# Attention pooling on one core: TensorE's loop from chunk 4 to the last, own places for two high halves of the odd chunks, and one softmax for the last two chunks

## The reference

```python
h = relu(einsum('bse,eh->bsh', behavior_emb, W_b) + (candidate_emb @ W_c)[:, None, :] + fc1_b)
scores = einsum('bsh,h->bs', h, fc2_w[:, 0]) + fc2_b[0]
attn = softmax(scores, axis=-1)
user_interest = einsum('bse,bs->be', behavior_emb, attn)
x = concatenate([user_interest, candidate_emb], axis=1)
logit = (relu(x @ mlp1_w + mlp1_b) @ mlp2_w + mlp2_b)[:, 0]
```

## Time and profile before

| | us |
|---|---|
| median of 3 runs | 272.15 (271.59 to 272.36) |
| the profiled execution | 271.89 |
| its span | 270.1 |
| TensorE busy in it | 255.4 (95%) |
| VectorE, ScalarE, GpSimd busy | 208.7, 198.1, 28.9 |

### The profile page before, as it was taken

How to read it: one execution, slowest core, us unless ns; L and a number is a source line. 1 busy time by engine, 2 the same in 40 slices (tenths; PEclk the granted TensorE clock), 3 DMA queues, 4 the chain that set the end, 5 groups by cost and what they waited for, 6 DMA issues and landing times.

```text
span 270.1 us, 10363 instructions
## 1 busy us (share of the span) xinstructions
PE 255.4 (95%) x3942; PEld 213.1 (79%) x3942; DVE 208.7 (77%) x321; ACT 198.1 (73%) x481; POOL 28.9 (11%) x38
## 2 busy tenths in 40 slices
PE   8979798979989999999999999999999999979995
PEld 7547677868778888888888988888888888868864
DVE  1448977958779797979899797979798897966441
ACT  2657975948859696978969696978879696966311
POOL 2000202011020110202020110202020101102100
PEclk9999999999999999999999999999999999999999
DMA  7999999999999999999999999999999999999200
GB/s 246 434 428 425 426 423 421 425 423 427 423 425 428 425 427 427 425 425 427 425 428 427 425 430 425 427 428 430 425 428 425 425 427 427 420 429 408 110 0 3
DMA packets 10688, 105.87 MB, mean 392 GB/s; under 512 B 1200, under 2 KB 1712, under 8 KB 2864
## 3 DMA queue, kind: packets, MB, share of 16 engines
q1 hardware_dynamic: 10384, 105.44, 92.8%
q10 hardware_dynamic: 288, 0.20, 0.2%
HBM read 105.63 MB, written 0.00 MB: 391 GB/s over the span
## 4 chain that ended last, share of the span: by engine, by line
PE 87%; DMA 4%; issue 3%; DVE 2%; SPq 1%; ACT 1%; DVEq 0%; ACTq 0%
PE z_ps L670 18%; PE s_ps L687 17%; PE z_ps L674 16%; PE z_ps L671 16%; PE u_ps L699 16%; DMA xt<-in_behavior_t 4%; PE z_ps L699 1%; PE z_ps L741 1%; PE z_ps L784 1%; SPq L260 1%; PE z_ps L778 1%; ACT hidden_rest L408 1%; DVE xl L498 1%; SPq L264 0%; PE z_ps L765 0%
## 5 line engine op out<-in xcount | busy, mean ns | idle before, releaser
L498 DVE TENSOR_TENSOR xl<-xt,xh 128x800 fp32r<-128x800 f32 x120 | 115.8, 996 | 6.1 <-ACT xh L364 3.3
L364 ACT CAST xh<-xt 128x800 fp32r<-128x800 f32 x120 | 102.3, 917 | 13.7 <-PE z_ps L674 10.8
L670 PE MATMUL z_ps<-xh,w_hi 128*128 128x512 f32 x240 | 86.0, 358 | 3.7 <-ACT hidden_rest L408 1.8
L671 PE MATMUL z_ps<-xh,w_lo 128*128 128x512 f32 x240 | 79.4, 345 | 0.0
L408 ACT ACTIVATE hidden_rest<-z_ps,bias 128x200 f32<-128x200 f32 x192 | 67.5, 454 | 7.6 <-PE z_ps L674 5.8
L674 PE MATMUL z_ps<-xl,w_hi 128*128 128x512 f32 x240 | 63.4, 345 | 0.5 <-DVE xl L498 0.5
L670 PEld LDWEIGHTS z_ps<-xh,w_hi 128*128 128x128 f32 x240 | 45.1, 188 | 21.2 <-issue 10.0
L508 DVE TENSOR_TENSOR hidden_rest<-z_ps,neg_bias 128x800 f32<-128x800 f32 x48 | 47.4, 987 | 9.7 <-PE z_ps L674 7.2
L335 POOL TENSOR_TENSOR weights_by_row<-weights,masks_sb 128x400 f32<-128x400 f32 x31 | 27.1, 873 | 224.1 <-DVE xl L498 194.4
L699 PE MATMUL u_ps<-x,weights_by_row 128*32 128x128 f32 (+1 forms) x1680 | 45.3, 262 | 6.0 <-issue 6.0
L671 PEld LDWEIGHTS z_ps<-xh,w_lo 128*128 128x128 f32 x240 | 45.1, 188 | 5.5
(11 more groups left out here) (70 smaller groups left out, 93.7 us busy)
## 6 DMA issues: line engine op xcount, KB each, us to landing
x<-in_behavior SPq DMA_DIRECT2D x31, 1600.0 KB, 18.5
xt<-in_behavior_t SPq DMA_DIRECT2D x30, 1600.0 KB, 16.8
xt<-in_behavior_t SPq DMA_DIRECT2D x4, 400.0 KB, 4.9
xt<-in_behavior_t SPq DMA_DIRECT2D x2, 800.0 KB, 7.6
x<-in_behavior SPq DMA_DIRECT2D x1, 832.0 KB, 8.3
x<-in_behavior SPq DMA_DIRECT2D x1, 768.0 KB, 9.7
later_sb<-in_later SPq DMA_DIRECT2D x1, 258.5 KB, 19.6
first_sb<-in_cand_rest SPq DMA_DIRECT2D x1, 192.0 KB, 5.7
```

What stands on the lines that cost most here:

```text
L364: nc.scalar.copy(xh[g][:, :], xt[q][:, g, :]).then_inc(xh_made, 1)
L498: nc.vector.tensor_tensor(xl[g][:, :], xt[q][:, g, :], xh[g][:, :].bitcast(F32), ALU.subtract).then_inc(xl_made, 1)
L670: nc.tensor.matmul(z[:, a:b], w_hi[:, :], xh[g][:, a:b], start=True, stop=False)
L671: nc.tensor.matmul(z[:, a:b], w_lo[:, :], xh[g][:, a:b], start=False, stop=False)
```

## The change

- `FIRST` is 4 instead of 6, so the loop's body starts at chunk 4. `periods` takes the number of turns: seven on TensorE (chunks 4 to 31, nothing is left behind it), six on ScalarE and VectorE (4 to 27; 28 to 31 are written out).
- TensorE has no `LAST` phase any more. Behind the loop it does the row sums, a transposition, the scores of 30 and 31 together, the weighted sums of 28 and 29, and then the end. The softmax of 30 and 31 is one of seven steps.
- Period 4 now has a transposition too, of a `pooled4` that GpSimd clears at the start; `pooled_t` has two pairs of columns more, and the counts of semaphores move by two.
- `xh` has two tiles more: the third and fourth high halves of odd chunks go there, and ScalarE casts all four of an odd chunk in one run, ahead of the exponentials.
- At the end the transposition of the pair 28, 29 is between the two sets of candidates, and on VectorE the last mask comes ahead of `normalise(0)`.
- Three tiles of the end (`inv_sel`, `pooled_n`, `z_all`) lie in buffers of `xt` that are free by then.

```diff
-        xh = [sb(f"xh{i}", [P, WIDTH], F32R) for i in range(GROUPS)]
+        xh = [sb(f"xh{i}", [P, WIDTH], F32R) for i in range(GROUPS + 2)]
...
-        FIRST = 6
+        FIRST = 4
...
-        def periods(body):
+        def periods(body, turns):
             def run(eng):
                 for c in range(FIRST):
                     body(c, c % X_BUFS, c)
-                with eng.Fori(0, (CHUNKS - FIRST - 2) // X_BUFS) as turn:
+                with eng.Fori(0, turns) as turn:
                     for j in range(FIRST, FIRST + X_BUFS):
                         body(turn * X_BUFS + j, j % X_BUFS, FIRST)
-                body(LAST - 1, (LAST - 1) % X_BUFS, FIRST)
-                body(LAST, LAST % X_BUFS, LAST)
+                for c in range(FIRST + turns * X_BUFS, CHUNKS):
+                    body(c, c % X_BUFS, LAST if c == LAST else FIRST)
...
+        def xh_of(q, g):
+            return xh[g if g < 2 or q % 2 == 0 else g + 2]
...
+            nc.gpsimd.memset(pooled4[:, :], 0.0).then_inc(pooled4_copied, 2)
...
-                    act.wait_ge(z_done, c * GROUPS + (g + 1 - GROUPS))
+                    act.wait_ge(z_done, c * GROUPS + (g + 1 - (GROUPS if g < 2 else 2 * GROUPS)))
...
-                if phase > 1:
-                    high_half(c, q, 3, None, phase == WHOLE)
                 if q % 2 == 1:
                     next_half(0)
                     biased_relu(c, q, 1, phase)
...
+                high_half(c, q, 3, None, phase == WHOLE)
                 biased_relu(c, q, 1, phase)
-                next_half(0)
-                next_half(1)
+                for g in range(GROUPS):
+                    next_half(g)
                 for n in range(2):
                     exponents(c - 2 + n, n, pair_steps(c - 2) + 2 * (PAIR_STEPS - 1 + n), phase == 2)
                 if phase > 2:
                     copy_pooled4(c - X_BUFS + 1, u_ps)
-                next_half(2)
                 biased_relu(c, q, 3, phase)
-            periods(period)(act)
+            periods(period, (CHUNKS - FIRST) // X_BUFS - 1)(act)
+            copy_pooled_t(LAST - 4, u_ps[:, P:P + 2 * ROWS])
+            for n in range(2):
+                exponents(LAST - 1 + n, n, pair_steps(LAST - 1) + 2 * (PAIR_STEPS - 1 + n), False)
             copy_pooled4(LAST - 2, u_ps)
             copy_pooled_t(LAST - 2, u_ps[:, P:P + 2 * ROWS])
-            exponents(LAST, LAST % 2, IN_PAIRS + 4 * ALONE_STEPS, False)
...
-            for n in range(ALONE_STEPS):
-                softmax(LAST, 1, n, IN_PAIRS + 2 * ALONE_STEPS, False)
+            for n in range(PAIR_STEPS):
+                softmax(LAST - 1, n, False)
+            mask_last()
             normalise(0)
-            mask_last()
...
-                    if phase == LAST:
-                        transpose_sums(LAST - X_BUFS, beside_z(q, g))
-                        score(LAST - 1, (q - 1) % X_BUFS, pair_steps(LAST - 3) + 2)
-                        weighted_sum(LAST - 3, (q - 3) % X_BUFS, False)
...
-            periods(period)(pe)
+            periods(period, (CHUNKS - FIRST) // X_BUFS)(pe)
             pe.wait_ge(later_loaded, 16)
             row_sums(0)
-            weighted_sum(LAST - 2, (LAST - 2) % X_BUFS, False)
-            score(LAST, LAST % X_BUFS, IN_PAIRS + 2)
-            transpose_sums(LAST - 2, u_ps[:, P:P + 2 * ROWS])
-            spread_inverses(0)
-            for part in range(2):
-                for m in range(2):
-                    mlp_candidates(part, m)
+            transpose_sums(LAST - 4, u_ps[:, P:P + 2 * ROWS])
+            score(LAST - 1, (LAST - 1) % X_BUFS, pair_steps(LAST - 3) + 2)
+            score(LAST, LAST % X_BUFS, None)
+            pe.wait_ge(pooled_t_copied, LAST - 1)
+            weighted_sum(LAST - 3, (LAST - 3) % X_BUFS)
+            weighted_sum(LAST - 2, (LAST - 2) % X_BUFS)
+            spread_inverses(0)
+            for m in range(2):
+                mlp_candidates(0, m)
+            transpose_sums(LAST - 2, u_ps[:, P:P + 2 * ROWS])
+            for m in range(2):
+                mlp_candidates(1, m)
             row_sums(1)
             weighted_sum_alone(LAST - 1)
```

More of the change, by code:

```diff
@@ L360, in high_half @@
                 if not early:
-                    act.wait_ge(z_done, c * GROUPS + (g + 1 - GROUPS))
-                nc.scalar.copy(xh[g][:, :], xt[q][:, g, :]).then_inc(xh_made, 1)
+                    act.wait_ge(z_done, c * GROUPS + (g + 1 - (GROUPS if g < 2 else 2 * GROUPS)))
+                nc.scalar.copy(xh_of(q, g)[:, :], xt[q][:, g, :]).then_inc(xh_made, 1)
             def exponents(c, buf, steps, early):
@@ L379, in copy_pooled_t @@
             def copy_pooled_t(c, summed):
-                act.wait_ge(pooled_t_done, c + 1)
-                nc.scalar.copy(pooled_t[:, bass.ds((c - 1) * ROWS, 2 * ROWS)], summed).then_inc(pooled_t_copied, 2)
+                act.wait_ge(pooled_t_done, c + 3)
+                nc.scalar.copy(pooled_t[:, bass.ds((c + 1) * ROWS, 2 * ROWS)], summed).then_inc(pooled_t_copied, 2)
             def bias_times_f2():
@@ L395, in biased_relu @@
                 act.wait_ge(z_done, c * GROUPS + (g + 1))
-                if g == 1 and phase == LAST:
-                    copy_pooled_t(LAST - X_BUFS, beside_z(q, g))
-                elif g == 1 and phase == FIRST and q % 2 == 0:
+                if g == 1 and phase == FIRST and q % 2 == 0:
                     copy_pooled_t(c - X_BUFS - 1, beside_z(q, g))
@@ L510, in biased_max, with softmax @@
                     nb.to_broadcast([P, TILES, EACH, PARTS]), ALU.max).then_inc(hidden_made, 1)
-            def softmax(c, buf, step, done, early):
-                n = 2 if buf is None else 1
-                mine = pair_runs() if buf is None else score_runs(buf).unsqueeze(1)
+            def softmax(c, step, early):
                 if step == 0:
-                    dve.wait_ge(scores_done, c + n)
+                    dve.wait_ge(scores_done, c + 2)
                     if not early:
[L521 to L525, removed]
+                        dve.wait_ge(weights_made, c)
+                    op = nc.vector.transpose(scores[:, :, :].rearrange("p c t -> p (c t)"), s_ps[:, 0:2 * RUN * Q])
                 else:
-                    dve.wait_ge(softmax_step, done + 2 * step)
+                    dve.wait_ge(softmax_step, pair_steps(c) + 2 * step)
                 if step == 1:
@@ L564, in normalise @@
                 dve.wait_ge(inv_done, part + 1)
-                dve.wait_ge(pooled_t_copied, b)
+                dve.wait_ge(pooled_t_copied, b + 2)
                 nc.vector.tensor_tensor(pooled_n[:, a * ROWS:b * ROWS], inv[:, 0:(b - a) * ROWS],
-                                        pooled_t[:, a * ROWS:b * ROWS], ALU.mult).then_inc(mlp_step[part], 1)
+                                        pooled_t[:, (a + 2) * ROWS:(b + 2) * ROWS], ALU.mult).then_inc(mlp_step[part], 1)
             negative_bias(0)
@@ L606, in period @@
                 for n in range(PAIR_STEPS):
-                    softmax(c - 2, None, n, pair_steps(c - 2), phase == 2)
+                    softmax(c - 2, n, phase == 2)
                 next_low(0)
@@ L611, in period @@
                 next_low(2)
-            periods(period)(dve)
+            periods(period, (CHUNKS - FIRST) // X_BUFS - 1)(dve)
             def mask_last():
@@ L669, in products @@
                 for a, b in halves:
-                    nc.tensor.matmul(z[:, a:b], w_hi[:, :], xh[g][:, a:b], start=True, stop=False)
-                    nc.tensor.matmul(z[:, a:b], w_lo[:, :], xh[g][:, a:b], start=False, stop=False)
+                    nc.tensor.matmul(z[:, a:b], w_hi[:, :], xh_of(q, g)[:, a:b], start=True, stop=False)
+                    nc.tensor.matmul(z[:, a:b], w_lo[:, :], xh_of(q, g)[:, a:b], start=False, stop=False)
                 pe.wait_ge(xl_made, c * GROUPS + (g + 1 - WHOLE * GROUPS))
@@ L711, in sum_tiles, with weighted_sum @@
                 return op
-            def weighted_sum(c, q, early):
+            def weighted_sum(c, q):
                 pe.wait_ge(x_loaded[q], loads(c, q))
                 pe.wait_ge(masked, c + 1)
-                if early:
-                    pe.wait_ge(shift_step, 1)
-                elif q % 2 == 0:
-                    pe.wait_ge(pooled4_copied, c)
+                if q % 2 == 0:
+                    pe.wait_ge(pooled4_copied, c + 2)
                 sum_tiles(c, q, u_ps, 0, WHOLE_TILES, GROUPS - 1).then_inc(pooled_done, 1)
@@ L820, in period @@
                         pe.wait_ge(masks_loaded, 16)
-                    if g != PHASE_AT or phase < 2:
-                        continue
-                    if phase == LAST:
-                        transpose_sums(LAST - X_BUFS, beside_z(q, g))
-                        score(LAST - 1, (q - 1) % X_BUFS, pair_steps(LAST - 3) + 2)
-                        weighted_sum(LAST - 3, (q - 3) % X_BUFS, False)
-                    elif q % 2 == 0:
+                    if phase == 3 and g == 3:
+                        pe.wait_ge(shift_step, 1)
```

(1 more changed line is left out.)

34 lines of the change are left out of this document (14 added, 20 removed).

## The result

| | before | after |
|---|---|---|
| median of 4 runs, side by side, us | 272.05 | 267.81 (267.65 to 267.95) |
| ratio, 95% interval | | 0.9845 (0.9828 to 0.9863) |
| span of the profiled execution, us | 270.1 | 266.1 |

The faster side was right, the size was not.

A forecast was written before the change was run, and what follows sets the result against it. TensorE, 87% of the chain, was taken as the bound, with time won only where it stands still. Terms -1.68 - 1.90 + 1.90 + 0.15 - 0.2 + 0.35 gave -1.4 us: 270.8 us predicted, range 268.8 to 272.0.

The forecast's parts named there:

- The faster side: The whole kernel: a measured time below 271.3 us, given a chance of 0.69.
- Steps 1 and 2: Loop from period 4, taking in period 30: stalls of 1.68 and 1.90 us go, a new 1.90 comes behind it.
- step 6: ScalarE casts four odd-chunk high halves in a row ahead of the exponentials, filling idle time; worth 0.
- my fourth rival: TensorE's loop is fetched again in each turn, stalling 1.68 us in each of 12 pairs: about 291 us; chance 0.01.
- Steps 3 to 5: Period 4's extra transposition, +0.15 us; scores of 30 and 31 together, -0.2; wait for ScalarE's copy near the end, +0.35.
- steps 2, 4 and 5: Period 30's stall gone, -1.90 us; new stall behind the loop, +1.90; last scores together, -0.2; wait for ScalarE's copy, +0.35.
- Slower through ScalarE: Steady loop: ScalarE's copy and relu late behind four casts, TensorE lacks a bank, 0.3 us a pair: 274.7 us; chance 0.08.
- DMA: Chunk 31's transposed block lands at 236.9 us; its cast waits 1.2 us, hidden behind the softmax with 2 us left.

The follow-up runs named there:

- e2: The changed kernel with the old places of the high halves and the old order of casts; 269.98 us against 271.61 before the change.
- e10: The changed kernel with 88 long-fulfilled waits added on TensorE behind the last quarter of chunk 1; 270.00 us against 271.38 before the change.
- e3: The changed kernel with an odd chunk's fourth cast back in that chunk's own period, ahead of its relu; 269.84 us against 271.61 before the change.
- e4: The changed kernel with the third and fourth casts moved behind the exponentials and the copy; 267.70 us against 271.61 before the change.
- e1: The kernel before with only the new places of odd chunks' high halves and the new order of casts; 267.79 us against 271.61.
- e8: The changed kernel itself, measured again as base on the chip of the lighter-traffic runs; 268.04 us against 272.01 before the change.
- e9: The changed kernel with small slow work of the end put between the weighted sums of 28 and 29 and around the transposition; 266.61 us against 271.38 before.
- e5: The kernel before, loading only half of each x block from chunk 4 on; 269.89 us against 272.01 with all loads.

## Why the prediction was wrong

- *Steps 1 and 2, the loop.* Right: period 8's stall went (1.69 of the 2.02, the rest is step 6), period 30's went (1.86 for 1.90; the pair should have won step 6's 0.35 besides, but took 15.07), a new one of 1.53 came after 70 sums, as counted, where I had charged 1.90. e2 has this part alone at -1.6.
- *The rule of the Trainium skill* ("Runtime: NRT & Kernel Launch", "Instruction fetch mechanics"), my fourth rival, did not come: seven turns, and no packet on q8 from 64 to 240 us. That section also has the next block fetched while the present one runs, and this mostly hidden. The trace agrees for packets among products (62.6 us in the change, no stall), and not for those in the sums: e10 shows the stall moving with the code, by 22 matmuls for 44 instructions, at up to 2.28 us.
- *Steps 3 to 5.* The end was +1.88 for +2.05 (steps 2, 4 and 5 together); the wait for ScalarE's copy is 0.3 for 0.35. The start was +1.12 for +0.15. Of the rest some 0.46 is the stretch at half clock; without it the same border is still 0.5 to 0.9 later in e2, e3 and e4 than before, where 0.15 is the transposition and, in e2 and e4, 0.2 a longer first stall; the remainder is open.
- *Step 6 failed: "TensorE waits for no cast in the steady loop, so this is worth 0".* It does not wait for the cast but for the relu behind the cast, 0.34 us a pair. Measured alone (e1) the step is worth 3.8 us, and e3 shows that it is the fourth cast's place that does it. With e1's 3.8 in its place the sum would have given 267.0, 0.8 below what came. The step looked at the casts that were added ahead of the exponentials, at their cover and at the idle time they fill (e4: of no account), and not at what leaves the odd chunk's period, the head of the diff.
- *Slower through ScalarE*, the third rival, had the mechanism right, a relu late behind casts, and the wrong sign: that was the state before.
- *DMA.* The block landed at 236.9 as forecast, but the shorter pairs had used up the lead: about 0.5 us of the change's time is the wait for blocks, which the sum had as hidden, and none in e8.
- *What stays open:* how far ahead a packet is asked for, the 14.83 of every second pair, and why the clock falls at 30 us in some executions and not in others.

## What to carry to other kernels

When a step leaves an engine's queue, ask first what stood behind it there, and when its inputs were ready; here the relu's were ready 0.7 us before it ran. TensorE's waits are read on both its rows, matmuls and weight loads: here many small "issue" on a weight load were a bank that came free late. And straight code that runs once, behind a loop, paid for its fetch here: wide matmuls where the new packet is due saved 1.0 us (e9).

## What the runs showed that was not expected

- A stall for instructions depends on the traffic of data: with the transfers idle the packet comes 2.8 us earlier and the stall is gone (e5).
- After TensorE had stood 1.6 us in two waits at 28 us its granted clock fell to the lower level, for 3.4 us, in five profiled executions and not in seven; in e10, one of the seven, it fell after the standstill of 2.28 us at 40 us. In the five TensorE had first had the full clock from 6.1 to 7.2 us, in the seven from 3.9 to 4.9. That tells the two groups apart; it isn't shown to be the cause.
- By the 22 matmuls that the stalls moved, each with its weight load, 88 fulfilled waits make TensorE's code 44 instructions longer. 176 of them make it stand 5.7 us longer at that place than in the change, while 88 cost nothing that stands out (2.0 us there, 1.8 to 1.9 in e1 to e4).
